# A decoder layer on one core: the ternary pass over the feed-forward weights starts eight steps later and stores through four places

## The reference

```python
def weight_quant(w):
    scale = 1.0 / jnp.clip(jnp.mean(jnp.abs(w)), EPS)
    wq = jnp.clip(jnp.round(w * scale), -1.0, 1.0) / scale
    return w + jax.lax.stop_gradient(wq - w)
x = x + self_attention(layernorm(x))
x = x + cross_attention(layernorm(x), ctx_2048)
x = x + h_bitlinear(silu(bitlinear(n, w_gate)) * bitlinear(n, w_up), w_down)   # n = layernorm(x)
```

## Time and profile before

| | |
|---|---|
| runs, us | 1656.93, 1656.32, 1654.77 (median 1656.32) |
| the profiled execution: its time, its span, us | 1656.29, 1654.4 |
| granted TensorE clock, mean share of 2.4 GHz | 0.985 |
| TensorE busy | 1566.2 us, 95% of the span |
| VectorE, ScalarE, GpSimd busy | 74%, 72%, 77% |
| self-attention phase | to about 612 us of the span |

### The profile page before, as it was taken

How to read it: one execution, slowest core, us unless ns; L and a number is a source line. 1 busy time by engine, 2 the same in 40 slices (tenths; PEclk the granted TensorE clock), 3 DMA queues, 4 the chain that set the end, 5 groups by cost and what they waited for, 6 DMA issues and landing times. The chain is left out here.

```text
span 1654.4 us, 23944 instructions
## 1 busy us (share of the span) xinstructions
PE 1566.2 (95%) x7520; PEld 1072.2 (65%) x7520; DVE 1222.6 (74%) x2240; ACT 1186.7 (72%) x1962; POOL 1271.4 (77%) x1138
## 2 busy tenths in 40 slices
PE   8899999999999987999999999999999878999996
PEld 4577777787787755666666666666656425666664
DVE  2489978878776756777877788788778556767765
ACT  2354567777544435999999889989999726877875
POOL 0387767787777723899999999999999928888880
PEclk9999999999999998999999999999999989999999
DMA  7224254332300004210311032102203130110000
GB/s 257 92 80 88 90 136 121 111 122 90 102 20 8 32 18 119 92 46 20 112 39 58 25 107 58 33 19 59 58 13 117 43 114 1 34 33 26 33 14 26
DMA packets 57190, 110.24 MB, mean 67 GB/s; under 512 B 9244, under 2 KB 13596, under 8 KB 56682
## 3 DMA queue, kind: packets, MB, share of 16 engines
q1 hardware_dynamic: 55488, 107.64, 21.2%
q10 hardware_dynamic: 1578, 1.07, 0.2%
HBM read 71.26 MB, written 18.88 MB: 54 GB/s over the span
## 5 line engine op out<-in xcount | busy, mean ns | idle before, releaser
L1374 POOL TENSOR_TENSOR x_p_lo<-x_p,x_p_hi 128x1024 fp32r<-128x1024 f32 x256 | 606.4, 2393 | 62.7 <-ACT x_p_hi L1176 38.4
L1308 DVE TENSOR_REDUCE x_maxes<-x_ps_a 128x1 f32<-128x1024 f32 x252 | 306.6, 1217 | 121.7 <-PE x_ps_a L1459 117.9
L1149 ACT ACTIVATE x_p<-x_ps_b,x_any_valid 128x1024 f32<-128x1024 f32 x256 | 285.1, 1114 | 57.3 <-PE x_ps_b L1439 52.5
L1176 ACT ACTIVATE x_p_hi<-x_p 128x1024 fp32r<-128x1024 f32 x256 | 271.4, 1060 | 6.4
L1439 PE MATMUL x_ps_b<-x_Q,x_K 103*128 103x512 f32 x512 | 216.6, 504 | 9.0 <-ACT x_p L1149 7.2
L1493 PE MATMUL x_ps_o<-x_p_hi,x_V 128*96 128x512 f32 x512 | 209.7, 410 | 4.2 <-POOL x_p_lo L1374 4.2
L1494 PE MATMUL x_ps_o<-x_p_lo,x_V 128*96 128x512 f32 x512 | 202.8, 396 | 0.0
L1459 PE MATMUL x_ps_a<-x_K,x_Q 99*128 99x512 f32 x504 | 168.0, 414 | 11.3 <-DVE x_maxes L1308 8.4
L440 ACT ACTIVATE a_aT_hi<-a_ps_a 128x512 fp32r<-128x512 f32 x64 | 38.3, 598 | 169.5 <-PE a_ps_a L723 146.3
L1439 PEld LDWEIGHTS x_ps_b<-x_Q,x_K 103*128 103x128 f32 x512 | 87.4, 190 | 99.6 <-issue 55.3
L1459 PEld LDWEIGHTS x_ps_a<-x_K,x_Q 99*128 99x128 f32 x504 | 88.8, 190 | 54.4 <-DVE x_maxes L1308 31.9
(11 more groups left out here) (263 smaller groups left out, 4007.3 us busy)
## 6 DMA issues: line engine op xcount, KB each, us to landing
shared<-in_L_ffn_w_gate SPq DMA_DIRECT2D x16, 512.0 KB, 4.3
shared<-in_L_ffn_w_up SPq DMA_DIRECT2D x16, 512.0 KB, 4.1
shared<-in_L_ffn_w_down SPq DMA_DIRECT2D x16, 512.0 KB, 4.4
shared<-in_ctx SPq DMA_DIRECT2D x8, 1024.0 KB, 8.0
x_scratch<-rows SPq DMA_DIRECT2D x31, 256.0 KB, 2.0
x_Q<-x_q_hi SPq DMA_DIRECT2D x112, 64.0 KB, 2.0
shared<-in_L_attn_out_w SPq DMA_DIRECT2D x6, 1024.0 KB, 8.2
ffn_quant<-shared SPq DMA_DIRECT2D x24, 256.0 KB, 4.5
```

The lines of the kernel that those rows point to most:

```text
L1149: act.activation(p[:, v % 3, :, :], ps_b[:, :, :], ACT.Exp, scale=any_valid[:, b % 2:b % 2 + 1]).then_inc(exp_ready, 1)
L1176: act.activation(p_hi[:, r], p[:, v % 3], ACT.Copy).then_inc(hi_ready, 1)
L1308: dve.tensor_reduce(out=maxes[:, c % 2, 3 + r:4 + r], in_=scores_bank(n)[:, :, :], axis=mybir.AxisListType.XY, op=ALU.max).then_inc(max_re ...
L1374: pool.tensor_tensor(out=p_lo[:, v % 3], in0=p[:, v % 3], in1=p_hi[:, r].bitcast(F32), op=ALU.subtract).then_inc(lo_ready, 1)
```

## The change

The ternary pass is moved eight steps later on every engine: ScalarE's round and clip to steps 24 to 47, VectorE's part to 25 to 48, SyncE's raw loads to rounds 22 to 45 and its stores to 26 to 49. The bf16 chunks go through four places in turn (columns 6144 to 8191) with four semaphores, so the clip of chunk k waits for the store of chunk k-4. The early loads for the cross-attention move from round 44 to round 52. Nothing is computed otherwise, and the pass of the sums stays where it is.

```diff
--- before.py
+++ after.py
@@ -155,7 +155,7 @@
         w2_raw = shared[:, 4096:8192].rearrange("p (s c n) -> p s c n", s=2, c=DC)
         f_abs = shared[:, 0:4096].rearrange("p (s n) -> p s n", s=4)
         f_raw = shared[:, 4096:6144].rearrange("p (s n) -> p s n", s=2)
-        f_quant = shared[:, 6144:7168].bitcast(BF16).rearrange("p (s n) -> p s n", s=2)
+        f_quant = shared[:, 6144:8192].bitcast(BF16).rearrange("p (s n) -> p s n", s=4)
         f_part = sb("f_part", [P, FFN_CHUNKS])
         f_sum = sb("f_sum", [P, 3])
         f_all = sb("f_all", [P, 3, P])
@@ -245,7 +245,7 @@
         out_made, x1_ready = sem("out_made"), sem("x1_ready")
         f_abs_in = [sem(f"f_abs_in{j}") for j in range(4)]
         f_raw_in = [sem(f"f_raw_in{j}") for j in range(2)]
-        f_stored = [sem(f"f_stored{j}") for j in range(2)]
+        f_stored = [sem(f"f_stored{j}") for j in range(4)]
         f_sum_out, f_all_in = sem("f_sum_out"), sem("f_all_in")
         f_part_ready, f_sum_ready, f_total_ready, f_mean_ready, f_scale_ready = (
             sem(n) for n in ("f_part_ready", "f_sum_ready", "f_total_ready", "f_mean_ready", "f_scale_ready"))
@@ -338,7 +338,7 @@
 
             def store_quant(k):
                 sp.wait_ge(f_quant_ready, k + 1)
-                sp.dma_start(ffn_quant[k // 8, :, k % 8 * 1024:(k % 8 + 1) * 1024], f_quant[:, k % 2, :]).then_inc(f_stored[k % 2], 16)
+                sp.dma_start(ffn_quant[k // 8, :, k % 8 * 1024:(k % 8 + 1) * 1024], f_quant[:, k % 4, :]).then_inc(f_stored[k % 4], 16)
 
             def store_sums(t):
                 sp.wait_ge(f_sum_ready, t + 1)
@@ -353,17 +353,17 @@
             for c in range(STEPS + 3):
                 if c + 2 < FFN_CHUNKS:
                     load_abs(c + 2)
-                if 0 <= c - 18 < FFN_CHUNKS:
-                    store_quant(c - 18)
-                if 0 <= c - 14 < FFN_CHUNKS:
-                    load_raw(c - 14)
+                if 0 <= c - 26 < FFN_CHUNKS:
+                    store_quant(c - 26)
+                if 0 <= c - 22 < FFN_CHUNKS:
+                    load_raw(c - 22)
                 if c in (9, 17, 25):
                     store_sums(c // 8 - 1)
                 if c in (11, 19, 27):
                     load_sums(c // 8 - 1)
-                if c == 44:
-                    for j in range(2):
-                        sp.wait_ge(f_stored[j], 16 * (FFN_CHUNKS // 2))
+                if c == 52:
+                    for j in range(4):
+                        sp.wait_ge(f_stored[j], 16 * (FFN_CHUNKS // 4))
                     sp.wait_ge(f_part_ready, FFN_CHUNKS)
                     fetch.early(sp)
                 if c == 57:
@@ -428,8 +428,8 @@
                 for m in merged_heads(c):
                     act.wait_ge(w12_made, m + 1)
                     act.activation(w12_hi[:, m, :], merge_bank(m), ACT.Copy).then_inc(w12_hi_ready, 1)
-                if 0 <= c - 16 < FFN_CHUNKS:
-                    k = c - 16
+                if 0 <= c - 24 < FFN_CHUNKS:
+                    k = c - 24
                     act.wait_ge(f_raw_in[k % 2], 16 * (k // 2 + 1))
                     act.wait_ge(f_scale_ready, k // 8 + 1)
                     act.activation(f_raw[:, k % 2, :], f_raw[:, k % 2, :], ACT.Copy, scale=f_scale[:, k // 8:k // 8 + 1], bias=MAGIC)\
@@ -452,12 +452,12 @@
                                        bias=neg_max[:, c % 2, j:j + 1], accum_out=row_sum[:, c % 2, j:j + 1]).then_inc(exp_ready, 1)
                     act.wait_ge(sink_arg_ready, c + 1)
                     act.activation(sink_exp[:, c % 2, :], sink_arg[:, c % 2, :], ACT.Exp).then_inc(sink_exp_ready, 1)
-                if 0 <= c - 16 < FFN_CHUNKS:
-                    k = c - 16
+                if 0 <= c - 24 < FFN_CHUNKS:
+                    k = c - 24
                     act.wait_ge(f_round_ready, k + 1)
-                    if k >= 2:
-                        act.wait_ge(f_stored[k % 2], 16 * (k // 2))
-                    act.activation(f_quant[:, k % 2, :], f_raw[:, k % 2, :], ACT.Relu, scale=-1.0, bias=f_clip[:, :])\
+                    if k >= 4:
+                        act.wait_ge(f_stored[k % 4], 16 * (k // 4))
+                    act.activation(f_quant[:, k % 4, :], f_raw[:, k % 2, :], ACT.Relu, scale=-1.0, bias=f_clip[:, :])\
                         .then_inc(f_clip_ready, 1)
                 t = tile_of(c, 8)
                 if t is not None:
@@ -502,10 +502,10 @@
                     dve.tensor_scalar(ln_bias[:, :], mv[:, 0:1], ln_rstd[:, :], -1.0, ALU.mult, ALU.mult).then_inc(bias_ready, 1)
                 for m in {-7: (0, 1, 2), -4: (3, 4), -3: (5, 6)}.get(c, ()):
                     split_part(m)
-                if 0 <= c - 17 < FFN_CHUNKS:
-                    k = c - 17
+                if 0 <= c - 25 < FFN_CHUNKS:
+                    k = c - 25
                     dve.wait_ge(f_clip_ready, k + 1)
-                    dve.tensor_scalar(f_quant[:, k % 2, :], f_quant[:, k % 2, :], 2.0, 1.0, ALU.min, ALU.subtract).then_inc(f_quant_ready, 1)
+                    dve.tensor_scalar(f_quant[:, k % 4, :], f_quant[:, k % 4, :], 2.0, 1.0, ALU.min, ALU.subtract).then_inc(f_quant_ready, 1)
                 t = tile_of(c, 6)
                 if t is not None:
                     dve.wait_ge(hT_hi_ready, t + 1)
```

## The result

The changed kernel takes 1644.74 us (median of 4 runs, 1642.38 to 1645.63), the kernel before 1655.55 beside it; the ratio is 0.9934 with a 95% interval of 0.9917 to 0.9951. That is 0.66% faster, 10.8 us, clear of the 0.2% that can be told apart, against a forecast of 1645.3 us.

A forecast was written before the change was run, and what follows sets the result against it. The prediction took TensorE as the bound, slowed in steps 18 to 34 by ScalarE's clips waiting for stores. 1656.29 us less 11.0 for four places, all other terms 0, gave 1645.3 us; range 1643.0 to 1649.0.

The forecast's parts named there:

- TensorE sets the pace: In clean self-attention stretches TensorE is busy all the time (99.24 of 99.24 us, steps 6 to 18); other engines' work hides underneath.
- the excess: Self-attention steps 18 to 34 take 140.91 us against 129.89 for the same kinds of tiles later: 11.0 us too much.
- the low clock: TensorE at 1.2 GHz instead of 2.4 from 233.1 to 239.9 us, after idling; claimed to cost 3.4 us.
- the sum of 10.9: TensorE's waits in steps 18 to 34 (5.8 + 1.7 + 0.4, less 0.4) plus 3.4 us for half clock, against 11.0 measured.
- rival (b): No change, 1656.3 us: two passes on VectorE at once, not ScalarE's waits, slow steps 18 to 34; chance 0.04.
- The four places bring -11.0, the move 0: Split of the gain: four store places end all 15.0 us of ScalarE's waits, -11.0 us; the pass eight steps later, 0.
- the loop: SyncE, held until a clip ends, issues the next raw load, then the store the next clip needs; only with two places.
- SyncE's queue: Waits for clips hold SyncE in steps 24 to 47 instead of 16 to 39; row stores and token loads unharmed: 0.
- the late raw load: Chunk 4's raw load, issued a step after the last sums, taken as in time: 0; if late, +1.0 us.
- Slower rival: In steps 40 to 47 round and clip delay the query copy and starve TensorE: up to +22.9 us, 1668.2; chance 0.04.
- Rival (d): Stores normally land in time (4.4 us), 9.8 us being one execution's; four places gain nothing: 1656.3 us; chance 0.02.
- Behind the phase: After self-attention everything shifts along; half-clock stretches at the phase change may add or take 1.7 us, taken as 0.

## Why the prediction was right, and where its parts were not

The total, its sign and its place were right. By the steps of the forecast:

- *TensorE sets the pace, and the excess is the 11.0 us of steps 18 to 34.* Right. The stretch lost 10.5 us, the tiles but for the second take what the clean ones took, and the clock no longer falls. Steps 34 to 50 are as long as before with eight more chunks: 129.9 us.
- *The clip's wait for a store, and the low clock behind it, make the excess.* Right for most: each of the three runs that end these waits or leave 3.7 us of them (four places, the earlier store, the move) takes 8.2 to 10.0 us out of the stretch. But the sum of 10.9 was too good. TensorE was busy in only 4.91 of the 6.80 us of low clock, which gives a cost of about 2.5 us and not 3.4; the rest was waiting, counted already. And one wait of 1.2 us in that sum, at the place below, does not come from a wait of the clip: the last clip before it that waited begins at 256.35, the next at 301.57. TensorE's timeline of the kernel before:
```profile
280.64 0.50 PE L653 MATMUL a_ps_out<-a_w_hi,a_aT_hi 128*128 128x512 f32 x1 [1.18 <-DVE a_aT_lo L551]
```
With four places it is still there (0.97 us at 272.70), with the pass moved it is gone. The trace of before already held the sign of rival (b).
- *The four places bring -11.0, the move 0.* This split failed, though the sum held. Alone, the places bring 8.4 us in the stretch and the move 9.95; together they bring 10.5. They are not two terms to add but two cures for one wait. What I had ruled out ("VectorE's relief in steps 16 to 23 takes nothing off", and against rival (b) "steps 16 to 18 have both passes and no loss") is worth 2.1 us: the two steps I looked at lie before step 18, and the loss falls in the two tiles behind it, where TensorE waits for line 551. I had argued from two steps to eight, and only one of the two has VectorE's ternary step, which begins in step 17. Rival (b) was thus wrong as a forecast and right as a term.
- *The write of the sums is why the first store is late, and the loop follows.* Half right. Behind the write a store lands in 8.8 to 11.8 us (the first one 9.8, against 7.6 without the write), and the write costs the tile from 26 to 30 its 1.1 us (34.06 before, 32.95 without it). But the loop needs no such push: without the write it starts at chunk 2 all the same. From one execution of each kernel, the 11.0 us split into 2.6 for the write with its low clock (140.9 to 138.3; without the write the clock is 1.00 throughout), 5.8 for the loop (138.3 to 132.5) and 2.6 for both passes side by side (132.5 to 129.9), of which the changed kernel keeps 0.5. "That loop exists only with two places" holds, since no clip waited with three or four, but two places are not enough for it: with two and the store issued first it does not exist. It takes the order clip, raw load, store, and stores slower than the 4.3 us that they need without the loads of the sums' pass.
- *SyncE's queue, the early fetch, the late raw load: 0.* Right. The raw load of chunk 4 was in time, 6.2 us after its issue, and line 435 waits for nothing.
- *Slower rival, decided from 1.4 us a step.* A further 1.15 us a step on ScalarE cost about 0.2 us a step. It was far.
- *Rival (d), and the rule of the Trainium skill beside it* ("DMA: Bandwidth & Descriptors", the anatomy of one DMA). I had left out that the Trainium skill gives this fit for transfers that GpSimd issues; here SyncE issues them. A store lands mostly in 3.5 to 4.8 us by itself, in 5.6 to 8.3 beside the loads of both passes, in 8.8 to 11.8 behind the sums' write. The measurements decide against the 2.6 us.
- *Behind the phase: 0, give or take 1.7.* In the profiled executions the phase ends 10.4 us earlier and the span is 11.6 us shorter; the other 1.2 us fell behind it, all of them in the feed-forward phase, where nothing was changed. The agreement of 1645.3 with 1644.7 has a part of luck in it: 0.5 us too much in the phase, a little given back behind, and parts of the program that nobody changed vary by more than that (last section).

The one thing left in the phase is the tile from 22 to 26, 33.46 us against 32.94 of its kind, lost in step 25 (8.44 us against 7.95 for its kind), where VectorE's first ternary step falls behind the first clip. TensorE waits 0.21 us for line 551 there, and VectorE had waited 0.37 us for the clip and 0.48 for the key copy of line 427 behind it on ScalarE. The extra ScalarE instruction of 1.15 us made TensorE's wait at that place 1.23 us, so the delay passes through ScalarE.

No version beats the changed kernel by what can be measured. The move with two places is as fast (0.9933 against 0.9934) with half the store buffer, and so is three places (0.9925); their intervals overlap.

## What to carry to other kernels

When an engine waits until a buffer is stored, read the issuing engine's program before adding buffers: here a store stood behind another wait in the same queue, and two places more, one line earlier, or the move away from the other pass each ended the loop or all but ended it. Price such a change by the stall it ends once, not once for each cure. And where two side tasks share an engine with the main work, judge the overlap by the tiles where both run through, not by the first steps of it.

## What the runs showed that I had not expected

The length of the phase change, from the first matmul of line 1408 to the first of line 1493, differs between kernels whose program is the same there. These are the stretches of the kernel before, then, each in its own fence, the changed one, the four places alone, and the move alone (columns as in rows 2):

```profile
612.19:656.29 44.10, 35.63 (x139) 22.88 (x139) 26.31 (x39) 20.28 (x26) 13.89 (x7) 0.88 0.36 92
```
```profile
601.77:645.65 43.88, 35.41 (x138) 23.31 (x139) 26.31 (x39) 20.27 (x26) 13.88 (x7) 0.88 0.38 96
```
```profile
602.99:645.29 42.30, 34.56 (x138) 21.79 (x139) 25.93 (x39) 20.27 (x26) 13.85 (x7) 0.92 0.35 90
```
```profile
602.78:643.84 41.06, 32.58 (x138) 21.17 (x139) 26.21 (x39) 20.25 (x26) 13.67 (x6) 0.96 0.37 96
```

With a mean granted clock of 0.88, 0.92 and 0.96 the same work takes 44, 42.3 and 41.1 us: up to 3 us depend on how long the clock stays at 1.2 GHz in this stretch, which is more than the difference between any two of the good versions in the phase that was changed, and more than the 1.7 us that I had allowed. It is not the change's doing: with only the fetch moved the stretch takes 42.3 us. The part from the first matmul of line 1873, in the feed-forward phase, to the end of the span varies as much, from 309.3 us (three places) to 312.6 (four places alone). A gain of a few us has to be read in the stretch where it arises. The 128 sums of four bytes each took 7.6 to 11.8 us in every run, and a 256 KB store issued right behind them landed 0.3 to 2.3 us after them.
